# An attention kernel: VectorE's score pairs move into ScalarE's three buffers

## What is computed

```python
xn = _layernorm(x, axis=-1)
x = x + attn(xn) + ffn(xn)

# attn, h = 16 heads of dh = 16 columns, s = 4096
q = _split_heads(query @ q_w.T + q_b, h) / scale
k = _split_heads(query @ k_w.T + k_b, h)
v = _split_heads(query @ v_w.T + v_b, h)
scores = jnp.einsum('bhqd,bhkd->bhqk', q, k)
attn = jax.nn.softmax(scores.astype(jnp.float32), axis=-1).astype(query.dtype)
ctx = jnp.einsum('bhqk,bhkd->bhqd', attn, v)
out = ctx @ out_w.T + out_b
```

## Time and profile before

| | us |
|---|---|
| median of three runs | 1961.22 |
| the profiled execution | 1961.78 |
| its span, first to last instruction | 1960.0 |
| first exponential of the heads (line 608) starts | 133.97 |
| a unit, 32 of them | 55.30 |
| ScalarE busy, whole span | 1812.5 |
| TensorE busy, whole span | 1912.2 |
| VectorE busy, whole span | 1274.3 |

### The profile page before, as it was taken

How to read it: one execution, slowest core, us unless ns; L and a number is a source line. 1 busy time by engine, 2 the same in 40 slices (tenths; PEclk the granted TensorE clock), 3 DMA queues, 4 the chain that set the end, 5 groups by cost and what they waited for, 6 DMA issues and landing times.

```text
span 1960.0 us, 39423 instructions
## 1 busy us (share of the span) xinstructions
PE 1912.2 (98%) x14963; PEld 687.3 (35%) x14963; DVE 1274.3 (65%) x1789; ACT 1812.5 (92%) x1993; POOL 44.2 (2%) x53
## 2 busy tenths in 40 slices
PE   5969999999999999999999999999999999999998
PEld 3623333333333333333333333333333333333337
DVE  6645765756566765756566765756566666656567
ACT  2339999999999999999999999999999999999991
POOL 2000000000000000000000000000000000000000
PEclk9979999999999999999999999999999999999999
DMA  7880111203021121203011121203011121203014
GB/s 198 270 250 3 25 31 26 31 10 47 9 34 15 25 31 26 31 10 47 10 31 18 25 31 26 31 10 47 9 27 22 25 31 26 31 10 47 10 21 109
DMA packets 65632, 83.87 MB, mean 43 GB/s; under 512 B 9952, under 2 KB 47360, under 8 KB 62208
## 3 DMA queue, kind: packets, MB, share of 16 engines
q1 hardware_dynamic: 65472, 81.58, 20.4%
HBM read 54.79 MB, written 26.21 MB: 41 GB/s over the span
## 4 chain that ended last, share of the span: by engine, by line
PE 93%; SPq 2%; DMA 1%; DVE 1%; ACT 1%; issue 1%; ACTq 0%
PE banks L1121 48%; PE banks L1100 36%; PE banks L1128 3%; PE banks L1011 2%; PE banks L1232 1%; PE banks L1022 1%; DVE o_sb L824 1%; ACT probs L608 1%; DMA k_parts<-probs 1%; PE banks L1058 1%; PE banks L1078 0%; DMA q_st<-q_parts 0%; PE banks L1216 0%; SPq L305 0%; PE banks L1224 0%
## 5 line engine op out<-in xcount | busy, mean ns | idle before, releaser
L608 ACT ACTIVATE probs<-banks 128x1024 f32<-128x1024 f32 x1920 | 1769.6, 1162 | 11.0 <-PE banks L1100 5.7
L1121 PE MATMUL banks<-probs,v_st 128*32 128x512 f32 x7680 | 1026.9, 607 | 5.6 <-DVE o_sb L824 5.4
L1100 PE MATMUL banks<-q_st,k_st 50*128 50x512 f32 x4096 | 814.4, 457 | 5.3 <-ACT probs L608 4.3
L1100 PEld LDWEIGHTS banks<-q_st,k_st 50*128 50x128 f32 x4096 | 361.2, 184 | 698.3 <-ACT probs L608 629.1
L856 DVE SCALAR_TENSOR_TENSOR horner<-horner,bits 128x1024 f32<-128x1024 f32 x256 | 313.6, 1225 | 8.8
L843 DVE TENSOR_SCALAR bits<-banks 128x512 int32<-128x512 f32 x256 | 176.9, 691 | 135.0 <-PE banks L1100 119.1
L1121 PEld LDWEIGHTS banks<-probs,v_st 128*32 128x32 f32 x7680 | 151.3, 108 | 321.1 <-issue 203.4
L824 DVE STREAM_TRANSPOSE o_sb<-banks 128x512 f32<-128x512 f32 x32 | 22.9, 717 | 311.6 <-PE banks L1121 311.6
L861 DVE SCALAR_TENSOR_TENSOR d_probs<-horner,powers 128x1024 f32<-128x1024 f32 x128 | 156.8, 1225 | 97.8 <-PE banks L1128 94.5
L852 DVE SCALAR_TENSOR_TENSOR horner<-bits 128x1024 f32<-128x1024 f32 x128 | 156.9, 1226 | 4.4
L1128 PEld LDWEIGHTS banks<-d_probs,v_st 128*32 128x32 f32 x2048 | 66.6, 110 | 153.2 <-issue 153.2
(11 more groups left out here) (90 smaller groups left out, 450.1 us busy)
## 6 DMA issues: line engine op xcount, KB each, us to landing
k_st<-k_parts SPq DMA_DIRECT2D x204, 128.0 KB, 4.4
q_st<-q_parts SPq DMA_DIRECT2D x204, 64.0 KB, 4.6
q_parts<-probs SPq DMA_DIRECT2D x9, 512.0 KB, 6.3
k_parts<-probs SPq DMA_DIRECT2D x9, 512.0 KB, 6.5
xnT_copy<-probs SPq DMA_DIRECT2D x8, 512.0 KB, 4.4
probs<-xnT_copy SPq DMA_DIRECT2D x8, 512.0 KB, 6.7
w_f<-xnT_copy SPq DMA_DIRECT2D x16, 256.0 KB, 5.3
out_dram<-horner SPq DMA_DIRECT2D x16, 256.0 KB, 2.1
```

The costliest lines, as they stand in the source:

```text
L608: act.activation(probs[:, at:at + WIDE * CHUNK].rearrange("p (t c) -> p t c", t=WIDE), banks[:, bank:bank + WIDE, :], ACT.Exp, scale=1.0 / ...
L1100: return pe.matmul(out, k_mm[rows, kt * P:(kt + 1) * P], blocks[rows, qb // GROUPS], start=True, stop=True)
L1121: last = pe.matmul(banks[VCOLS * qb:VCOLS * (qb + 1), 6, :], v_st[:, kt, :], probs[:, at:at + CHUNK], start=first_one, stop=last_one, tile ...
```

## The change

VectorE's pairs are no longer scored into a bank of their own. The 64 pairs of a unit have one order of **places**, 0 to 63; all are scored into the three buffers in turn. Five of them, at the places 10, 22, 32, 42 and 52 (`D_AT`), are taken by VectorE and not by ScalarE: the four pairs of the rows 15 and 31 and one of the two pairs of row 30. VectorE reads a pair from PSUM in one instruction of 1024 columns, and a new semaphore, `d_taken`, frees the buffer; the score pair three places on waits for `d_taken` or for `exp_done`. ScalarE exponentiates the other 59.

All 32 rows are summed in the same way, four matmuls of 512 columns, one row a round, one round after its scores; a row's two pairs are waited for separately. The rows whose pairs VectorE computes are summed later than their scores stand. The quarter sums are gone. Units alternate between two accumulators, banks 6 and 7, and the sampled maxima of the next unit are computed in the other unit's bank, in rounds 6 and 7. VectorE turns the negated maxima itself by one transpose in blocks of 32, so that TensorE's turning of them goes; the rows come out in four pieces, and 16 DMAs carry them for four. The first 128 columns of k are loaded by six DMAs of their own. On VectorE the loop over heads is written out.

```diff
-    D_ROWS = (KT // 2 - 1, KT - 1)
-    D_SLOTS = ((2, 4, 6, 14), (16, 24, 34, 36))
-    D_SUM = ((27, 29, 31, 33), (49, 51, 53, 55))
+    D_AT = (10, 22, 32, 42, 52)
+    D_PAIRS = ((KT // 2 - 1, 0), (KT // 2 - 1, 1), (KT - 1, 0), (KT - 1, 1), (KT - 2, 0))
+    MAX_ROUNDS = (6, 7)
+    AE = PAIRS - D_BLOCKS
...
             def load_rows(c, u, count):
                 sp.wait_ge(c.row_ready, count)
                 for i in range(PARTS):
                     for g in range(GROUPS):
-                        sp.dma_start(q_st[at:at + 1, u * UG:(u + 1) * UG].rearrange("o (t c) -> o t c", c=P),
-                                     neg_row[i * UT + g * GT:i * UT + (g + 1) * GT, :]).then_inc(c.row_in[u], 16)
+                        at, r0 = g * GROUP + KROWS + i, i * UT + g * GT
+                        to = q_st[at:at + 1, u * UG:(u + 1) * UG].rearrange("o (t b x) -> o b t x", t=GT, x=PARTS * UT)
+                        for b in range(BLOCKS):
+                            first_row = b * PARTS * UT + r0
+                            sp.dma_start(to[:, b], neg_row[first_row:first_row + GT, :]).then_inc(c.row_in[u], 16)
...
+                def d_block(h, u, n):
...
+                    dve.wait_ge(c.st_done, h * HP + (pair + 1))
+                    dve.tensor_scalar(words.rearrange("p (t c) -> p t c", t=WIDE), banks[:, bank:bank + WIDE, :],
+                                      -EXP_BIAS, EXP_BIAS, ALU.max, ALU.add).then_inc(c.d_taken, 1)
...
+                def buffer_free(h, n):
...
+                    if p in D_AT:
+                        pe.wait_ge(c.d_taken, h * HD + (D_0 + back * HD + u * D_BLOCKS + D_AT.index(p) + 1))
+                    else:
+                        pe.wait_ge(c.exp_done, h * HE + (EXP_0 + back * HE + u * AE + A_INDEX[p] + 1))
...
+                def weighted_sum(h, u, at):
+                    kt = SUM_ROWS[at]
...
+                    for j in range(QB // WIDE):
+                        if (kt, j) in D_PAIRS:
+                            n = D_PAIRS.index((kt, j))
+                            pe.wait_ge(c.d_ready, h * HD + (u * D_BLOCKS + n + 1))
+                            src = d_probs[:, n % 2 * HALF:(n % 2 + 1) * HALF]
+                        else:
+                            a = u * AE + A_INDEX[PLACE[kt, j]]
+                            pe.wait_ge(c.exp_done, h * HE + (EXP_0 + a + 1))
...
+                def sampled_heads():
+
+                    for r in range(HEADS * HP // 2):
+                        nxt = [divmod(n, HP) for n in (2 * r + LEAD, 2 * r + LEAD + 1) if n < HEADS * HP]
...
+                        for i, (h, n) in enumerate(nxt):
+                            scores(h, n)
...
+                        if r:
+                            unit, at = divmod(r - 1, KT)
+                            weighted_sum(unit // UNITS, unit % UNITS, at)
```

More of the change, by code:

```diff
@@ L252, in program @@
         ACC_0 = 1
+        D_0 = 1
         OUT_0 = 16
@@ L281, in program @@
[L281 to L291, removed]
+        ORDER = []
@@ new lines, in program @@
+        HALF_0_READ = max(p for p, (kt, j) in enumerate(ORDER) if kt < KT // 2)
+        FIRST_READ = max(p for p, (kt, j) in enumerate(ORDER) if kt == 0)
+        SUM_ROWS = []
+        for s_at in range(KT):
+            left = [kt for kt in range(KT) if kt not in SUM_ROWS]
+            SUM_ROWS.append(min(left, key=lambda kt: max(PLACE[kt, j] + (12 if (kt, j) in D_PAIRS else 0)
+                                                         for j in range(QB // WIDE))))
+        SUM_AT = {kt: s_at for s_at, kt in enumerate(SUM_ROWS)}
@@ L293, in program, with sums_before_reuse, span @@
+        SUMMED = [1 + max(SUM_AT[kt] for kt in range(half * (KT // 2), (half + 1) * (KT // 2))) for half in range(2)]
+        def sums_before_reuse(a):
+            before, a = divmod(a - SLOTS, HE)
+            u, a = divmod(a, AE)
+            return before * STEPS + u * KT + SUM_AT[ORDER[A_PLACES[a]][0]] + 1
+        def span(start, count):
+            return slice(start, start + count) if isinstance(start, int) else bass.ds(start, count)
         tok = "(t p) d -> p t d"
@@ L937, in outputs @@
+                if c.full:
+                    with dve.Fori(0, HEADS) as h:
+                        head_full(h)
+                else:
+                    for h in range(HEADS):
+                        head_sampled(h)
+                dve.wait_ge(c.chain, HEADS * HEAD_LINKS + c.links_0)
             def outputs(again):
@@ new lines, in scores @@
+                def scores(h, n):
+                    u, p = divmod(n, PAIRS)
+                    kt, j = ORDER[p]
+                    bank = WIDE * ((n if c.full else h * HP + n) % BUFS)
+                    blocks = q_mm[:, u * UG:(u + 1) * UG].rearrange("k (c j x) -> k j c x", j=QB // GROUPS, x=P)
+                    buffer_free(h, n)
+                    for g in range(GROUPS):
+                        rows = slice(g * GROUP, g * GROUP + STACK)
+                        last = pe.matmul(banks[:, bank + g, :], k_mm[rows, kt * P:(kt + 1) * P], blocks[rows, j],
+                                         start=True, stop=True)
+                    last.then_inc(c.st_done, 1)
@@ L1194, in attend @@
[L1194 to L1200 removed]
+                            max_part(0, g, 0, 1)
+                    for n in range(LEAD):
+                        if n:
+                            pe.wait_ge(lo_done, LO_0 + 4 * NCH - 2 * (2 - n))
+                        arrivals(0, n)
+                        scores(0, n)
```

460 lines of the change are left out of this document (212 added, 248 removed).

## The result

The changed kernel takes 1984.51 us (median of 4 runs, 1983.53 to 1988.13) against 1959.77 of the kernel before (median of 4 runs, 1954.82 to 1961.71); the ratio is 1.0134, with a 95% interval of 1.011 to 1.0157. It is slower by 1.3%; 1988 was predicted. The profiled execution took 1983.53 us, its span is 1981.7.

What follows compares the result with a forecast made beforehand. ScalarE's exponentials were taken as the bound, TensorE close behind. The profiled 1961.8 + 18.6 (loop) + 8.5 (start) = 1988.9, less 0.6 to the runs' median, gave 1988 us; eight in ten runs from 1950 to 2008.

Steps and rivals of the forecast that it cites:

- The pace: ScalarE sets the pace in the loop: 59 exponentials a unit for 60, at 0.9165 us each, 54.07 us.
- The chain: From exponential p-3's end through a whole sum to p+1's end: 3.04 us against 2.75, stalling ScalarE 0.29 at each VectorE place.
- Place 22: After two parts of the maxima TensorE is 0.46 us late at this place, so the stall is 0.65 us.
- The unit: One loop repeat: 54.07 + 4 x 0.29 + 0.65 = 55.88 us against 55.30, 18.6 us longer over 32 units.
- VectorE: Five pairs for four, a block taken as 7.7 us; it keeps up and frees the bank 1.8 us after the scores.
- rival D: VectorE comes late to its pairs and holds the bank; a block of 8.8 us gives 2000 us; chance 5%.
- The sums' second wait: Each sum's new wait in its middle, for its row's second pair; expected to cost nothing visible, TensorE's round staying at 1.66.
- rival C: Each sum's mid-wait costs 0.1 us, TensorE becomes the bound, unit 56.8 us, 2018 us in all; chance 7%.
- The start: SyncE's extra loads delay the saves and the first exponential to near 142 us: bounds 0 and 12, taken 8.5 us.
- A: No stall at VectorE places, the buffers' slack swallows it: unit 54.1 to 54.4 us, 1936 us in all; chance 13%.

Runs made afterwards that it cites:

- experiment 1: The changed kernel with its five VectorE places moved to the odd places 11, 23, 33, 43, 53: 1980.25 us, ratio 1.0096 to the kernel before.
- 2: The changed kernel with four VectorE places a unit (10, 22, 32, 42) for five: 2004.11 us, ratio 1.0219 to the kernel before.
- experiment 8: The changed kernel with VectorE's pairs scored as single tiles into the unused accumulator bank, sums spread over the 59 exponentials: 1974.62 us, ratio 1.0075.
- 4: The changed kernel with VectorE places at 16, 26, 36, 46, 56 and the maxima in rounds 5 and 6: 1985.22 us, ratio 1.0122.
- experiment 5: The changed kernel with VectorE places at 18, 28, 38, 48, 58 and the maxima in rounds 4 and 5: 1996.32 us, ratio 1.0178.
- Experiment 6: The changed kernel with six VectorE places (11, 21, 31, 41, 51, 59), maxima in rounds 5 and 12, VectorE's part behind its second block: 2009.37 us.
- experiment 9: experiment 8 with tiles, maxima and sums spread out, quantisation in the even unit, first sixteen row loads issued by GpSimd: 1949.51 us, ratio 0.9942.
- experiment 7: The changed kernel with the sixteen row loads ahead of the first unit issued by GpSimd instead of SyncE: 1980.20 us, ratio 1.0104.

## Why the prediction was right, point by point

- **The pace.** 0.9165 us per exponential and 59 of them: met, 0.917 at every place without a stall.
- **The chain.** Right in each link (0.43, 0.99, 0.55 us) and in its sum: 0.30 measured at four places for 0.29. Shown by experiment 1 (it moves with the place), 2 (one place less, one stall less) and 8 (out of the buffers, no such stall). The Trainium skill, "TensorE: Matmul & The Clock Gate", Part 2, says that matmuls stay in program order. For this chain the traces agree: in none does a score pass a sum. At the maxima they do not: in the changed kernel's trace, behind each of the 62 parts of the maxima from 200 us on, a score matmul of the pair that follows has a recorded start up to 0.07 us before that of the part's last matmul. Nothing in the chain hangs on this.
- **Place 22.** 0.65 expected at one exponential; the loss is 0.57 behind place 22 and 0.08 at place 19, already inside the span. The prediction's 0.46 us of lateness doesn't follow from its own 10.8 and 10.4. These give 0.40 and a stall of 0.58, which is what place 22 shows; that 0.65 is also the two losses together is luck. Experiments 1, 4 and 5 show the cause is the maxima's 0.6 us and how many plain rounds follow.
- **The unit.** 55.88 predicted, 55.92 measured. Over 32 units the 0.61 more in each (55.917 for 55.303, mean of 31) are 19.6 us for 18.6.
- **VectorE.** The first operation takes 1225 ns for the whole pair, and a block 766.14 to 773.86, 7.72 us, for 7.7 taken. The Trainium skill, "VectorE: DVE Perf Modes", "Why PSUM operands drop a tier", says that fp32 from PSUM runs at the lowest rate, and the trace agrees: 1225 ns against 695 for line 863 on as many columns of SBUF. The block is that of the earlier trace rows with one operation for two. It waits for its scores at every block, so rival D is wrong; D's price was wrong as well, since 0.9 us a unit for a block of 8.8 gives some 2017 us and not 2000. VectorE frees the bank 1.77 us behind the scores, as predicted, and place 13 is scored 3.26 behind them (765.60 to 768.86), not 2.8, so the cover is larger. Experiment 6 shows how near the edge it is: a sixth block fills it.
- **The sums' second wait** costs nothing: plain rounds are 1.66 us (776.10 to 777.76 between scores), so rival C is wrong.
- **The start** was the term that was mis-sized. SyncE's part was right: sixteen loads in 11.09 us where the earlier trace rows has four in 2.93, and the first exponential at 141.76 for 142 predicted. SyncE's issues and ScalarE's timeline after the change:

```profile
123.36 11.09 SPq L427 DMA_DIRECT2D q_st<-neg_row  x16
134.50 0.44 SPq L366 DMA_DIRECT2D q_parts<-probs  x1
...
141.76 6.52 ACT L630 ACTIVATE probs<-banks 128x1024 f32<-128x1024 f32 x7 [9.32 <-DMA k_parts<-probs]
149.01 3.01 ACT L630 ACTIVATE probs<-banks 128x1024 f32<-128x1024 f32 x3 [0.73 <-PE banks L1134]
```

What I left out is what happened behind the first exponential before the change: ScalarE's timeline of the kernel before, and four windows with the granted clock (the column behind the engines' busy times), two of before and two of after:

```profile
139.38 1.94 ACT L608 ACTIVATE probs<-banks 128x1024 f32<-128x1024 f32 x2 [0.73 <-PE banks L1100]
142.82 1.94 ACT L608 ACTIVATE probs<-banks 128x1024 f32<-128x1024 f32 x2 [1.50 <-PE banks L1100]
146.26 1.94 ACT L608 ACTIVATE probs<-banks 128x1024 f32<-128x1024 f32 x2 [1.50 <-PE banks L1100]
149.70 1.94 ACT L608 ACTIVATE probs<-banks 128x1024 f32<-128x1024 f32 x2 [1.50 <-PE banks L1100]
```
```profile
144.00:148.00 4.00, 4.00 (x21) 1.03 (x13) 3.86 (x5) 2.50 (x3) 0.00 (x0) 0.50 0.00 0
148.00:152.00 4.00, 4.00 (x24) 1.00 (x16) 3.09 (x3) 2.14 (x3) 0.00 (x0) 0.59 0.00 0
```
```profile
139.00:144.00 5.00, 1.04 (x4) 0.54 (x4) 0.00 (x0) 2.24 (x3) 0.00 (x0) 0.50 0.98 364
148.00:152.00 4.00, 4.00 (x28) 1.15 (x24) 0.70 (x1) 3.23 (x4) 0.00 (x0) 0.79 0.21 66
```

Before the change TensorE worked through its stretch at 1.2 GHz (half the 2.4 of the rest), and two exponentials took 3.44 us for 1.83: the first unit was 61.58 us long, 6.3 more than the others. In the changed kernel TensorE is at the same clock while it has nothing to do (1.04 us busy in 5), and its first unit loses 1.25. So 7.8 us of later start give 5.0 back, and the term is 2.8 for 8.5. With 19.6 for the loop and 0.7 less at the end that is 21.7, by which the spans differ; the prediction had 27.1 for it. Four traces line up, with the granted clock of each: the first unit's excess is 6.3, 3.35, 1.6 and 1.25 us where 17.3, 12.6, 8.6 and 7.9 us of half clock lay behind the first exponential (before, experiment 9, experiment 7, after). In the seven others 7.4 to 10.3 us of it stand beside an excess of 0.6 to 2.3.

The chances were sound in direction; A, the strongest rival at 13%, rested on ScalarE losing only 0.31 us a unit before, but there the chain had a whole exponential more to lie under.

## What to carry to other kernels

When work is taken off an engine that is fed through a ring of buffers, follow the chain from the freed buffer to the next use: a skipped place shortens what covers it by one item, and a producer that is 97% busy can't make it up; its reserve is never more than the ring. Here the answer was to send the skipped work through another buffer and to keep the producer's extra jobs apart. And look at the first unit of a loop by itself: a later start may fall on time that was lost anyway.

## What the runs showed of the hardware

A sum of four column-tiled matmuls on 256 columns takes 0.57 us for 1.00 at 512, and a lone pair between two sums 0.43 for 0.33, so small pieces cost TensorE 0.4 us per split.

In experiment 5 one wait of 1.45 us for a load was followed by half clock. TensorE's timeline and two windows:

```profile
489.12 0.31 PE L1078 MATMUL banks<-k_st,q_st 48*128 48x32 bf16 x6 [1.45 <-DMA q_st<-q_parts]
```
```profile
486.00:490.00 4.00, 2.55 (x26) 0.88 (x28) 0.58 (x4) 3.50 (x5) 0.00 (x0) 0.99 0.64 93
490.00:496.60 6.60, 6.60 (x36) 1.73 (x32) 0.00 (x0) 3.67 (x4) 0.00 (x0) 0.50 0.00 0
```

That unit is 60.08 us long for 55.55. Twelve other waits at this place, of 0.22 to 1.39 us, were not followed by it in this trace; what tells them apart stays open. At the end of experiment 8 TensorE's wait of 2.67 us for VectorE was followed by it too, from 1918.4 to 1925.2 us.
